# Probability transposes on two row halves of the array, in a shifted-window attention block

## The reference

```python
xn = layernorm(x, ln1_w, ln1_b)
xs = jnp.roll(xn, shift=(-SHIFT, -SHIFT), axis=(1, 2))
# cut into windows of 49 tokens: xw [-1, 49, C]
qkv = xw @ qkv_w + qkv_b                     # split into q, k, v of 6 heads
attn = jnp.einsum('bhqd,bhkd->bhqk', q, k) * scale
attn = jax.nn.softmax(attn, axis=-1)
o = jnp.einsum('bhqk,bhkd->bhqd', attn, v)
o = o @ proj_w + proj_b                      # back to the image, rolled back
x = shortcut + o
h = layernorm(x, ln2_w, ln2_b)
h = jax.nn.gelu(h @ mlp_w1 + mlp_b1, approximate=False)
x = x + (h @ mlp_w2 + mlp_b2)
```

## Time and profile before

| | |
|---|---|
| median of three runs | 3045.3 us (3044.94 to 3047.61) |
| profiled execution | 3046.47 us |
| its span | 3044.7 us |
| TensorE busy | 2996.3 us, 98% |
| TensorE weight loads busy | 2857.5 us, 94% |
| VectorE busy | 2376.0 us, 78% |
| ScalarE busy | 2306.3 us, 76% |
| GpSimd busy | 1483.4 us, 49% |
| mean granted TensorE clock | 0.992 of full speed |

### The profile page before, as it was taken

The page is one execution under the profiler, slowest core; times in us unless marked ns, Lnnn a source line. Parts: engine busy times, 40 slices in busy tenths (PEclk is TensorE's granted clock), DMA queues, the critical chain, the costliest instruction groups (busy, mean ns, idle before and its releaser), DMA issues.

```text
span 3044.7 us, 114197 instructions
## 1 busy us (share of the span) xinstructions
PE 2996.3 (98%) x43444; PEld 2857.5 (94%) x43444; DVE 2376.0 (78%) x6416; ACT 2306.3 (76%) x4493; POOL 1483.4 (49%) x1550
## 2 busy tenths in 40 slices
PE   5999999999999999999999999999999999999998
PEld 5999999999999999999999999999999999999997
DVE  4778877887887788788778878877887788788775
ACT  2777777777777777777777777777777777777776
POOL 1454455445445544544554454445445544544553
PEclk7999999999999999999999999999999999999999
DMA  1000100010011001001100100010010001001100
GB/s 46 26 24 24 29 26 24 25 30 24 24 27 28 24 24 31 25 24 27 29 24 24 30 26 24 26 29 24 24 29 26 24 26 29 24 24 28 28 24 17
DMA packets 112145, 79.78 MB, mean 26 GB/s; under 512 B 10128, under 2 KB 111602, under 8 KB 112114
## 3 DMA queue, kind: packets, MB, share of 16 engines
q1 hardware_dynamic: 112114, 79.35, 9.7%
HBM read 40.78 MB, written 38.54 MB: 26 GB/s over the span
## 4 chain that ended last, share of the span: by engine, by line
PE 97%; SPq 1%; DVE 1%; ACT 0%; issue 0%; POOL 0%; DMA 0%; DVEq 0%; POOLq 0%; ACTq 0%
PE ps L803 35%; PE ps L806 16%; PE ps L878 6%; PE ps L910 5%; PE ps L832 5%; PE ps L883 5%; PE ps L929 4%; PE ps L884 4%; PE ps L880 4%; PE ps L879 4%; PE ps L766 3%; PE ps L774 2%; PE ps L895 2%; PE ps L898 1%; SPq L286 1%; PE ps L776 1%
## 5 line engine op out<-in xcount | busy, mean ns | idle before, releaser
L383 POOL TENSOR_TENSOR gl<-g,gh 128x392 fp32r<-128x392 f32 x768 | 789.5, 1050 | 251.6 <-ACT gh L668 251.3
L803 PE MATMUL ps<-zh,w 128*128 128x392 f32 x3072 | 715.0, 348 | 0.6 <-ACT zh L630 0.6
L803 PEld LDWEIGHTS ps<-zh,w 128*128 128x128 f32 x3072 | 533.9, 189 | 31.4 <-ACT zh L630 0.8
L263 POOL TENSOR_TENSOR prob<-prob,rcp 128x588 f32<-128x588 f32 x128 | 152.2, 1189 | 537.0 <-DVE rcp L558 537.0
L413 DVE BATCH_NORM_STATS2 st<-xin 98x6 f32<-98x192 f32 x512 | 145.8, 348 | 328.1 <-DMA xin<-in_x 327.9
L662 ACT ACTIVATE g<-ps,biasf 128x392 f32<-128x392 f32 x768 | 389.3, 574 | 3.1 <-PE ps L803 3.0
L366 POOL TENSOR_TENSOR xb<-xin,projbv 98x768 f32<-98x768 f32 x128 | 234.5, 1832 | 296.2 <-DVE z L426 266.2
L803 PE MATMUL ps<-zh,wqkv 128*128 128x400 f32 x1536 | 378.1, 355 | 0.0
L668 ACT ACTIVATE gh<-g 128x392 fp32r<-128x392 f32 x768 | 365.1, 533 | 0.0
L803 PEld LDWEIGHTS ps<-zh,wqkv 128*128 128x128 f32 x1536 | 289.9, 190 | 2.5
L806 PE MATMUL ps<-wqkv,zh 128*114 128x192 f32 x2048 | 289.5, 269 | 0.4 <-issue 0.4
(11 more groups left out here) (105 smaller groups left out, 7234.2 us busy)
## 6 DMA issues: line engine op xcount, KB each, us to landing
xin<-in_x SPq DMA_DIRECT2D x128, 147.0 KB
out<-yo SPq DMA_DIRECT2D x128, 147.0 KB
xin<-in_x SPq DMA_DIRECT2D x128, 71.2 KB
out<-yo SPq DMA_DIRECT2D x128, 71.2 KB
xin<-in_x SPq DMA_DIRECT2D x128, 54.8 KB
out<-yo SPq DMA_DIRECT2D x128, 54.8 KB
xin<-in_x SPq DMA_DIRECT2D x128, 18.8 KB
out<-yo SPq DMA_DIRECT2D x128, 18.8 KB
```

What stands on the lines that cost most here:

```text
L383: pool.tensor_tensor(gl[:, m, :], g[:, m, :], gh[:, m, :].bitcast(F32), ALU.subtract)\
L803: last = pe.matmul(dst, cols(w, part), act_ if zh is zh2 else windows(act_, WIDE, EVEN), start=(n == 0), stop=(n == 4))
```

## The change

Each transpose of 113 partitions becomes two of 49 partitions, against the two 49 x 49 diagonal blocks of the identity. The upper one (partitions 0 to 48, `e = 0`) and the lower one (64 to 112, `e = 1`) address different row halves of the array. The two of a pair write different banks: in the first quarter of a half the upper ones write the half's first bank and the lower ones its second, and in its second quarter (`swapped`) it is the other way round. The order is quarter 0 of half 0, quarter 0 of half 1, then quarter 1 of half 0, quarter 1 of half 1. Before each quarter 1 TensorE waits until the first quarter of the same half has ended (`pt_first`), and all waits stand on an instruction of their own (`nop`).

```diff
+        pt_first = sem("pt_first")
         pt_done = sem("pt_done")
...
             def turn_probs(i):
 
+                def quarter(half, swapped):
+
+                    for n in range(TILES // 4):
+                        for e in range(2):
+                            j = e ^ swapped
+                            b = TILES // 2 * half + TILES // 4 * j + n
+                            q = slice(64 * e, 64 * e + TOK)
+                            last = pe.transpose(ps[:, TP[half] + j, 128 * n + 64 * e:128 * n + 64 * e + TOK],
+                                                prob[q, 2 * b:2 * b + 2, :].rearrange("p w k -> p (w k)"), ident[q, q])
+                    return last
+
                 wait(pe, v_ready, 1, i, 1)
                 for half in range(2):
                     wait(pe, p_norm[half], 1, i, 1)
                     if feeds(i):
                         wait(pe, g_done, KC, i - 1, 2 * half + 2)
-                    for n in range(TILES // 2):
-                        b = TILES // 2 * half + n
-                        last = pe.transpose(ps[:, TP[half] + n // 3, 128 * (n % 3):128 * (n % 3) + PAIR],
-                                            prob[0:PAIR, 2 * b:2 * b + 2, :].rearrange("p w k -> p (w k)"),
-                                            ident[0:PAIR, 0:PAIR])
-                    last.then_inc(pt_done, 1)
+                    pe.nop(nofuse=True)
+                    quarter(half, 0).then_inc(pt_first, 1)
+                for half in range(2):
+                    wait(pe, pt_first, 2, i, half + 1)
+                    pe.nop(nofuse=True)
+                    quarter(half, 1).then_inc(pt_done, 1)
```

## The result

The changed kernel takes 3064.22 us (median of 5 runs, 3062.0 to 3064.77) against 3046.48 us before (5 runs): a ratio of 1.0059, 95% interval 1.0048 to 1.0070. It is slower by 18 us. The forecast was slower, with 3054 us and a range of 3036 to 3100; the loss that it gives is 8.9 us, half of what was measured.

What follows compares the result with a forecast made beforehand. TensorE, busy 98% of the span, was taken as the bound. A loss of 0.07 us in each of 127 groups gave 8.9 us on the 3045.3 us median: 3054 us, range 3036 to 3100.

Steps and rivals of the forecast that it cites:

- The bound and the place: TensorE, busy 98%, bounds the kernel; the loss arises where MLP2's first load waits for ScalarE's copy of half 0.
- the sign that was named: Expected in the new profile: a new idle of TensorE before MLP2's first load, released by ScalarE's copy.
- The round: Two transposes, upper and lower row half, bound by their weight load: r = 0.056 us, between 0.041 and 0.084.
- The halves at work together: Weight loads of two row halves overlap in transposes; the second of a pair starts 0.01 us after the first.
- (C): Rival: each half's load costs an untiled full load, r = 0.11 us; loss 0.46 us a group, 3103 us; chance 8%.
- (D): Rival: halves don't run together, 24 transposes follow each other at 0.056 us; loss 0.47 us a group, 3105 us; chance 7%.
- The sum along the bank: Half 0 complete at 0.96 instead of 0.74 us, MLP2's first load at 1.82 instead of 1.75: 0.07 us lost a group.
- 4r + 2w - 0.354: Predicted loss in us per group; r is a round of two transposes, w TensorE's wait after a producer's end, 0.10 us.
- TensorE's own path: Z transposes start at 1.12 us, 0.04 earlier than before; worth nothing because MLP2 then waits for the bank.
- The saving of 0.6 us of array time: Array time saved by the split transposes, said to go into two changeovers, the own-result wait and late hand-over.
- What I costed at nothing: Waits for normalised probabilities and GELU, due long before; 0.1 us if GELU's cover were gone. ScalarE's later chain is hidden.
- rival (A): The hand-over to MLP2 is hidden: 4r + 2w between 0.306 and 0.402, time 3045 to 3048 us; chance 25%.

Runs made afterwards that it cites:

- short copy: ScalarE copies only 17 of 49 queries of half 0: against the change 3048.73 us, against the kernel before 3046.36 us.
- the halves in order: The change with both quarters of half 0 ahead of those of half 1: 3117.96 us, ratio 1.0246 to the kernel before.
- a bank for each row half: The change with upper transposes writing a half's first bank, lower ones its second, without quarters or waits for own results: 3025.6 us.
- The order without the wait: The kernel with a bank for each row half, put in the change's order of quarters, no wait between: 3042.77 us, ratio 0.9994.
- the narrow weights: The kernel with a bank for each row half, 64 instead of 128 weight columns per transpose after the first group: 3002.4 us.

## Why the prediction was right, and where it was off

**The bound and the place: right.** The loss is made in one place, and MLP2's first load follows the end of half 0's copy by a constant 0.12 us where it had 0.25. The short copy on the change and on the kernel before shows that this hand-over is the cause of 15 of the 18 us. One reason was put wrong: half 0 was to be late because a quarter of half 1 stands between its parts and because of the wait. With the halves in order the copy starts no earlier, so the wait alone makes it late. And the sign that was named, an idle of TensorE before MLP2's first load, is not listed; only the distance to the copy's end shows the wait.

**The round.** Predicted 0.056, measured 0.062 between pairs: in the kernel with a bank for each row half, 24 transposes with loads of 128 columns, two at a time, start within 0.74 us (0.96 - 0.22), 0.10 for the first round with its load in the open, then ten of 0.062 to 0.063, and under 0.01 within the last pair. With 64 columns it fell to 0.042. The rule of the Trainium skill, "TensorE: Matmul & The Clock Gate", section "LDWEIGHTS (loading the stationary operand)", would have made it 0.107, by the estimate in the prediction; the trace disagrees with it for transposes of this type. Its other half, that the rows don't matter, agrees: the record of one load is 138 ns for 49 rows, 140 for 98 and 141 for 113.

**The halves at work together: right.** Rivals (C) and (D) fall: they put the last transpose 1.2 and 1.3 us after the first, and in the change, with its waits, it starts 0.90 us after it (1.12 - 0.22).

**The sum along the bank: the term that was too small.** It gave 0.07 us a group, or 8.9 us; measured are 0.145 and 18. Laid beside the trace piece by piece:

- Each of the two waits, the third quarter's for the first and MLP2's for the copy, takes 0.12 us and not 0.10: 0.04 in all.
- The third quarter takes 0.42 us from its first load to its end (1552.67 to 1553.09, the end of the record that starts at 1552.87), where 0.385 was forecast: 0.03. After a wait the lower transposes trail the upper ones by 0.03 us and not by 0.01, and one transpose lasts 0.22 us and not 0.207.
- The first quarter takes 0.39 us instead of 0.385. Its rounds start 0.01 earlier than forecast and its records are 0.015 longer.
- The copy's start behind half 0's end (0.10) and its length (0.66) were right.

With r = 0.062 and w = 0.12 the prediction's own form, 4r + 2w - 0.354, gives 0.134 us or 17.0 us. That it comes so near is partly luck: the longer transposes, which it leaves out, are nearly made up by rounds that it takes too long in the first quarter. The direction is as clear as it is because the terms missed to the same side: at the forecast of 0.07 us the loss was only 0.02 above the 0.048 that the prediction itself could tell from no change.

**TensorE's own path: wrong in sign.** I had the z transposes start at 1.12, 0.04 earlier than before, with their load ahead of that start. Measured, the last probability transpose starts at 0.98 instead of 0.92 from when the first was due, for the same longer wait and third quarter; the first z load follows 0.15 later, at 1.14, and is in the open: that transpose lasts 304 instead of 248 ns. Counted with this load, as in the forecast, the z transposes start at 1.19, 0.03 later than the 1.16 before. The short copy shows it: some 3 us over before with the hand-over out of the way. The saving of 0.6 us of array time that the prediction names is 0.49 by its own round (1.16 - 12 x 0.056); nothing else in it rests on this.

**What I costed at nothing: right.** The second quarter started on pace behind the first, so the GELU wait cost nothing. ScalarE's idle before its next results fell from 0.29 us to 0.15 (the line of 1557.19) and stayed above zero, so its later chain was hidden.

**What rival (A) was.** The order without the wait comes to the same: no change in time, and the bank still the limit.

The change was laid out so that both row halves share both banks of a half. That asked for the swap, the quarters and the wait. The gain of the row halves was there all along, 20 us, and what the layout asked for lost it: taken one after the other, 17 us by the order and 19 by the wait.

## What to carry to other kernels

Before packing small matmuls into row halves, choose the output layout so that each row half has banks of its own; here a wait of TensorE for its own result took 0.34 us from the start of the last transpose to the next load (0.22 until its record ended, and 0.12). Other work put into such a wait did not delay half 0, and it saved about 55 us: by so much the halves in order are slower than the change. Without a wait the same order put half 0 off by 0.19 us and lost 17 us. When a stage gets shorter, look at who waits for its first result, not at its length: here equal TensorE time in two orders differed by 17 us. For a short transpose, ask what its weight load costs: here that, and not the 49 columns streamed, set the pace.

## What the runs showed of the hardware

- Neighbours that use the same row half do not keep the other half idle: with six upper transposes ahead of six lower ones, 24 starts took 0.90 us and not the 1.4 of 24 rounds, and transposes started in another order than that of the program.
- A transposing load of 128 fp32 columns on half of the rows goes every 0.062 us and one of 64 columns went every 0.042, with both row halves loading at once.
- Entering the tiled form cost 0.09 us, as before the products of probabilities and values. Leaving it took 0.15 us from the last start to the next load, plus 0.056 for the load in the open, where it is 0.14 behind the scores, although here only the rows are split. With the narrow weights it was 0.13.
- A hole of 0.15 us in TensorE's work is not listed among its waits; the 0.58 us record of twelve transposes with the next load at 1552.67 is all that shows it.
